# GpSimd's part in a fused cross-attention and coupling-network kernel: low halves in other slots, and five of eight token couplings made on GpSimd

## What is computed

```python
gf = _global_net(x.mean(axis=1, keepdims=True), ...)          # one number for each batch
out = x
for _ in range(3):
    tf = _coupling_net(out, ...)                              # one number for each token
    combined = 0.7 * gf + 0.3 * tf
    coupling = 0.1 + adaptive_range * (combined - 0.5) * 2.0
    out = out + coupling * _twist(out)                        # twist: swap quarters, two of them negated
```

## Time and profile before

| | us |
|---|---|
| median of 3 runs | 1073.47 (1073.15 to 1073.99) |
| the profiled execution | 1072.12 |
| its span, first to last instruction | 1070.2 |
| busy: PE, DVE, ACT, POOL | 977.3, 843.8, 901.5, 573.9 |
| mean granted TensorE clock | 0.983 of full speed |

### The profile page before, as it was taken

One profiled execution on the slowest core, in us unless ns is written; L12 is line 12 of the kernel. 1 busy time (PEld: TensorE's weight loads), 2 busy tenths in 40 slices (PEclk: granted clock), 3 DMA queues, 4 the chain that ended last, 5 costly groups with the idle time before them and its releaser, 6 DMA issues.

```text
span 1070.2 us, 21910 instructions
## 1 busy us (share of the span) xinstructions
PE 977.3 (91%) x7260; PEld 526.2 (49%) x7260; DVE 843.8 (79%) x1770; ACT 901.5 (84%) x1121; POOL 573.9 (54%) x1053
## 2 busy tenths in 40 slices
PE   6899999999899999999999999999989999996993
PEld 4456435554355544555445543555435554454431
DVE  3888796997879886987869879699796988688485
ACT  3999778997799978998789977899779997895575
POOL 3366604876068740887228870487606874087204
PEclk7999999999999999999999999999999999999897
DMA  5433002430033200432005310153002430020002
GB/s 118 88 59 58 6 2 44 103 88 1 1 75 89 71 1 1 98 89 48 1 1 118 88 30 1 36 112 88 0 2 69 92 74 1 2 54 31 11 1 80
DMA packets 191119, 51.71 MB, mean 48 GB/s; under 512 B 165920, under 2 KB 174624, under 8 KB 191008
## 3 DMA queue, kind: packets, MB, share of 16 engines
q1 hardware_dynamic: 191008, 50.31, 22.2%
HBM read 33.37 MB, written 16.78 MB: 47 GB/s over the span
## 4 chain that ended last, share of the span: by engine, by line
PE 43%; DVE 16%; POOL 14%; ACT 13%; issue 10%; SPq 2%; DMA 1%; DVEq 0%; POOLq 0%; ACTq 0%
PE ps L1255 8%; PE ps L1269 7%; PE ps L1239 6%; PE ps L1159 5%; ACT probs L914 5%; PE ps L1190 4%; ACT probs L920 3%; PE ps L1175 3%; POOL f_hat L470 3%; PE ps L1278 2%; POOL twisted L525 2%; DVE move_u L780 2%; DVE move_u L801 2%; DVE move_v L782 2%; POOL q_hat L449 2%
## 5 line engine op out<-in xcount | busy, mean ns | idle before, releaser
L914 ACT ACTIVATE probs<-ps,u_scale 120x2048 f32<-120x2048 f32 x128 | 253.7, 1982 | 23.2 <-PE ps L1159 23.2
L920 ACT ACTIVATE probs<-probs,exp_bias,clip 120x2048 f32<-120x2048 f32 x128 | 270.2, 2111 | 0.1
L1269 PE MATMUL ps<-h,w 128*128 128x512 f32 x384 | 185.5, 605 | 14.5 <-ACT h L948 13.8
L1159 PE MATMUL ps<-q_t,k_t 32*120 32x256 f32 x2048 | 148.9, 405 | 21.5 <-ACT probs L914 20.6
L489 POOL TENSOR_TENSOR c<-tok_c 128x16 f32<-128x16 f32 x8 | 1.8, 223 | 277.8 <-issue 277.8
L1190 PE MATMUL ps<-wo_t,of_t 128*128 128x256 f32 x512 | 143.5, 403 | 1.0 <-DVE xy L717 1.0
L692 DVE STREAM_TRANSPOSE o_t<-ps 128x512 f32<-128x512 f32 x128 | 90.6, 708 | 68.0 <-PE ps L1175 67.7
L1175 PE MATMUL ps<-probs,va 120*32 120x256 f32 x2048 | 138.7, 389 | 1.6 <-ACT probs L920 1.5
L1159 PEld LDWEIGHTS ps<-q_t,k_t 32*120 32x120 f32 x2048 | 93.4, 180 | 58.7 <-issue 51.4
L1269 PEld LDWEIGHTS ps<-h,w 128*128 128x128 f32 x384 | 67.5, 189 | 93.0 <-issue 66.0
L1190 PEld LDWEIGHTS ps<-wo_t,of_t 128*128 128x128 f32 x512 | 86.9, 189 | 49.9 <-issue 41.7
(11 more groups left out here) (132 smaller groups left out, 1791.5 us busy)
## 6 DMA issues: line engine op xcount, KB each, us to landing
xy<-in_x_dram SPq DMA_DIRECT2D x64, 256.0 KB, 3.3
out_dram<-xy SPq DMA_DIRECT2D x64, 256.0 KB, 2.1
cbuf<-in_ctx_dram SPq DMA_DIRECT2D x64, 120.0 KB, 2.8
va<-in_ctx_dram SPq DMA_DIRECT2D x64, 120.0 KB, 3.6
tok_c<-coup SPq DMA_DIRECT2D x256, 0.5 KB, 2.0
move_v<-in_L_xattn_W_out_dram SPq DMA_DIRECT2D x1, 256.0 KB, 5.2
move_u<-in_L_ffn_cn_w_dram SPq DMA_DIRECT2D x1, 256.0 KB, 3.3
w<-in_L_ffn_cn_w_dram SPq DMA_DIRECT2D x1, 128.0 KB, 3.1
```

The source lines that it names most:

```text
L914: eng.activation(probs[:, b % 2, n * HALF:(n + 1) * HALF, :].rearrange("k h q -> k (h q)"), banks(SCORE_BANK, 4)[0:KEYS, :], ACT.Tanh, sca ...
L920: eng.activation(p, p, ACT.Exp, scale=clip[0:KEYS, 0:1], bias=exp_bias[:, b:b + 1]).then_inc(s_exp, 1)
L1159: last = eng.matmul(banks(SCORE_BANK + r)[0:KEYS, odd * S:(odd + 1) * S], k_t[rows, b % 2, odd, n, :], q_t[rows, b % 2, n, :], start=True, ...
L1269: last = eng.matmul(banks(bank), w2[:, k, :], h1[:, p % 2, k, :], start=(k == 0), stop=(k == EK - 1))
```

## The change

GpSimd's low halves of chunks 0 and 1 move from slots 2, 3, 5, 6 to slots 2, 4, 4, 7: of the two in slot 4 one comes right behind the feature norm, the other at the end. And `COUPLE_DVE` = 3: VectorE makes the couplings of updates 0, 1 and 2, GpSimd those of updates 3 to 7, by the same two instructions, between its feature norm of slot 0 and the coefficients. Arithmetic, DMAs and all the other queues are as they were.

```diff
-        LOW_AT = (2, 3, 5, 6)
+        LOW_FIRST = {4: (0, 1)}
+        LOW_LAST = {2: (0, 0), 4: (1, 0), 7: (1, 1)}
+        COUPLE_DVE = CHUNKS - 1
...
+            def couple_beside(g, p):
+
+                turn, chunk = UPDATES * g + p, slot_of(p)[1]
+                eng.wait_ge(s_th, turn + 1)
+                eng.wait_ge(s_gcs, g + 1)
+                eng.wait_ge(s_coup, CB * turn)
+                for b in range(CB):
+                    c = coup[:, turn % 2, b * S:(b + 1) * S]
+                    eng.tensor_scalar(c, c, c_tok[:, 0:1], c_batch[:, chunk * CB + b:chunk * CB + b + 1],
+                                      ALU.mult, ALU.add).then_inc(s_coup, 1)
...
                     norm_2(i - LAG)
+                if place(i) in LOW_FIRST:
+                    low_half((i - LAG) // GROUP, *LOW_FIRST[place(i)])
                 if after_ffn(i):
+                    for p in range(COUPLE_DVE, UPDATES):
+                        couple_beside(groups_before(i) - 1, p)
                     coefficients(groups_before(i) - 1)
...
-                if place(i) in LOW_AT:
-                    part = LOW_AT.index(place(i))
-                    low_half((i - LAG) // GROUP, part // EK, part % EK)
+                if place(i) in LOW_LAST:
+                    low_half((i - LAG) // GROUP, *LOW_LAST[place(i)])
+            for p in range(COUPLE_DVE, UPDATES):
+                couple_beside(NGROUPS - 1, p)
             coefficients(NGROUPS - 1)
...
                     for p in range(CHUNKS):
-                        couple(i, p)
+                        if p < COUPLE_DVE:
+                            couple(i, p)
                         update_both(i, p)
                     for p in range(CHUNKS, UPDATES):
-                        couple(i, p)
                         update_u(i, p)
```

## The result

The changed kernel is slower: 1076.13 us (median of 9 executions, 1075.8 to 1078.9) against 1073.15 for the kernel before in the same measurement. The ratio is 1.0034, with a 95% interval of 1.0023 to 1.0044; on 1073.15 that is 3.6 us (2.5 to 4.7). The predicted time was 1073.9 in a range of 1068.5 to 1078.3. So the time lies in the range, but past the 0.2% that I had called "same", and past the forecast's own range by 0.5 us.

A forecast was written before the change was run, and what follows sets the result against it. In feed-forward, VectorE's updates were taken to hold pass 10's second layer, which sets each group's end. Couplings +1.1 us and low halves -0.7 summed to +0.4, so 1073.47 became 1073.9 us, range 1068.5 to 1078.3.

The forecast's parts named there:

- The bound: Feed-forward stage: the start of pass 10's second layer on TensorE, 543.12, sets the group's end.
- Update 3: Its coupling pair on GpSimd, hidden by nothing, runs 527.2 to 528.3; the moves start 0.5 us later.
- Update 4 and the Gelu of pass 8: VectorE reaches update 4 at 533.95 against 533.90; pass 8's Gelu comes 0.15 us later.
- The size of a half: A GpSimd coupling half takes 1.5 us beside back-to-back VectorE work, 0.55 when VectorE idles; a pair 2.8 us.
- the first rival: GpSimd gets in only when VectorE stops: +4.8 us, with the low halves' move 1077.6; chance 0.22.
- Updates 5 and 6: Update 5's moves 0.1 us earlier; update 6's tanh 0.4 earlier, its moves at 540.35 against 540.26.
- Update 7: Comes 0.4 us later, but its Gelu still precedes TensorE's turn: hidden, except in the last group.
- Part two: Moving the low halves to slots 2, 4, 4, 7 in attention: -0.1 us a group, taken as -0.7 us.
- part one: Five couplings, updates 3 to 7, move from VectorE to GpSimd: +0.1 x 8 + 0.3 = +1.1 us.
- The starved case: Couplings wait for a whole VectorE update, first halves over 2 us; update 6 is 0.55 us later; chance 0.22.
- The whole-instruction lock: VectorE loses the whole 0.55 us per coupling half; update 6 +1.4 us a group, about 1084; chance 0.05.
- The queue really shortens: Coupling pairs near 1.1 to 2 us: -0.3 to -0.7 us a group, 1068 to 1071; chance 0.21.

The follow-up runs named there:

- couple_imm: `couple_only` with GpSimd's coupling instruction taking two constants, 0.05 and 0.1, and no columns; sixth stage 58.19 us against 58.59 before, one execution.
- couple_onecol: `couple_only` with the coupling's scale read from its column and the offset the immediate 0.1; sixth stage 58.42 us against 58.59 before, one execution.
- low_only: The kernel before with only the low halves moved, to slots 2, 4, 4, 7; VectorE makes all couplings; ratio to before 1.0008.
- couple_only: The kernel before with only the couplings of updates 3 to 7 moved to GpSimd, low halves in their old slots; ratio to before 1.0031.
- shadow: The kernel before plus two coupling-form GpSimd instructions on a scratch tile behind each tanh of updates 4 to 7, nobody waiting for them; ratio 1.0068.
- before_rows4: The kernel before with coupling rows in four buffers and four semaphores instead of two, all couplings on VectorE; ratio to before 0.9983.

## Why the prediction was right or wrong

*The bound.* Right: TensorE's second layer of pass 10, held by VectorE's updates through the Gelu, sets the stage's end. It came 0.34 later, and the stage 0.45.

*Update 3.* Right: alone 1.10 us, the moves 0.42 later than before (predicted +0.5). It is one of the two dear steps, +0.34 of the stage.

*Update 4 and the Gelu of pass 8.* Right in number by luck (+0.12 against +0.15). I had VectorE come last, at 533.95, held up by 0.34, and the coupling done by 533.5. VectorE was held up by 0.1 only and free at 533.72, and the pair, 3.35 us and not 2.8, ended at 533.99: two errors met in the same place, and update 4 waited for GpSimd, not for VectorE's own queue.

*The size of a half.* **The step that failed: the length of a coupling half on GpSimd under VectorE's updates.** I took "1.5 us for an instruction while VectorE runs back to back", and four boundaries for a pair, from two normalizations of the same form at 257.30 and 513.92. The halves took 1.34 and 2.02 in update 4, and 2.00 and 0.98 in update 5, the same to 0.02 us in all eight groups. A pair is 3.35 us, not 2.8. `couple_imm` and `couple_onecol` show what it hangs on: the two column operands, without which a half takes 0.97 at most. That each is one more wait for a boundary is inferred. The two rows were of the right form, and no instruction of it in that trace lasted over 1.575 us; why they got through sooner than the 2.0 us of updates 4 and 5 is not shown. The forecast took the longest rows there for the rule and left all that lies above them to the first rival.

*Updates 5 and 6.* Wrong for that reason, twice over. With coupling 4 ending at 533.99 instead of 533.5, GpSimd starts coupling 5 only behind it (the 0.20 in its row), so update 5 is 0.1 late and not 0.1 early. And the rows of coupling 4 land later, so the tanh of update 6 is 0.12 late and not 0.4 early. By the prediction's own steps this 0.5 us passes on to coupling 6 (whose pair was shorter than I had it, 1.79 us for 2.05) and to update 6: +0.34 instead of +0.1. In size this is the whole miss at pass 10: (0.34 - 0.1) x 8 = 1.9 us.

*Update 7.* Wrong: "hidden" it was not. I compared its Gelu with TensorE's turn for pass 11 (546.6 against 547.1), and that part held, as the second layer of pass 11 has no wait. But on ScalarE the second Gelu of pass 10 and the next slot's logits stand behind this Gelu in the queue, so all of its 0.58 us is passed on to them (552.00 - 3.82 = 548.18, was 547.60), and some of it to the last cycle's tanh: the stage ends 0.45 late, not 0.34. This is 0.1 x 8 = 0.9 us. The step asked only who reads the late result, not who is queued behind it.

*Part two.* I had given it 0.1 us a group. `low_only` shows that much for an attention stretch, the changed kernel does not (68.45 us against 68.40 in `couple_only`); ScalarE's idle time is unchanged, as I said. The net was wrong. My row at 507.81 showed that a low half, with its two inputs, can double a VectorE instruction, and I used it only against part one. In slot 7 the moved half did this to `o_n`, and a stage in each of the two kernels was 1.3 to 1.8 us longer behind it.

*The sum.* Part one was to cost 0.1 x 8 + 0.3 = 1.1 us and costs 0.45 x 8 = 3.6 (0.42 x 8 = 3.4 in `couple_only`), part two was to give 0.7 back and gives nothing that can be measured (1.0008, 0.9998 to 1.0017): +0.4 has become +3.6.

*The rivals.* The starved case named +0.55 a group for update 6, and asked for first halves over 2 us. Measured were 1.34, 2.00, 1.25, 1.52 and +0.34: the outcome lies between it and the forecast. The rule of the Trainium skill ("SBUF — State Buffer", "Who interferes with whom") is that the engine which issues first holds the port for its whole length. GpSimd's two-input low half comes near it: `o_n`, begun 0.1 us behind a low half of 1.16, took 1.60 us where it takes 0.70 in the same place of `couple_only`. The couplings do not bear it out: `shadow` shows 0.14 to 0.2 us lost for an instruction that takes 0.55 alone. The whole-instruction lock would have made `shadow` 1.015 or more; it was 1.0068. "The queue really shortens" was true of updates 4 and 5 alone (-0.26 us).

What stays open: how often part two's collision comes, and part of the spread of the last attention stretch, 59.4 to 62.1 us from kernel to kernel. The other part is the clock. In that stretch the granted clock is at its lower level (1.2 GHz) for 6.8 us in eleven traces and for 10.2 us in the three with the longest stretches, 61.7 to 62.1; the 1.9 us between 59.4 (the changed kernel) and 61.2 (before), both with 6.8, are not explained.

## What to carry to other kernels

Before an instruction is handed to a second engine, write down three times for it: when its input is ready, when its reader is free, and how long it lasts *under the stream beside which it will run*; it pays where the lead between the first two covers the third, and here it did for one half (1.8 us) and not for two (3.35). Fewer column operands shorten the last of the three: two less took a half from 2.02 to 0.97 us at most. Splitting a pair so that GpSimd's half was done before VectorE's own took the gain that moving it whole gave away (0.9976 against 1.0011 for updates 4 to 7). And a late result can cost twice: its reader, and everything queued behind the instruction that waits for it.

## What the hardware showed

- On GpSimd a 128x256 `tensor_scalar` beside back-to-back VectorE work takes up to 0.97, 1.47 and 2.02 us with no, one and two column operands, and 0.40, 0.47 and 0.55 alone. Before the result I had given the columns no part in it.
- Each such instruction costs VectorE 0.14 to 0.2 us in `shadow`, where it lasts 0.58 to 2.02 us itself. In the changed kernel ten of them cost VectorE 0.3 us in a whole stage.
- A two-input GpSimd instruction of 1.16 us that started 0.1 us ahead of a VectorE one made that one last 1.60 and 1.65 us instead of 0.97 or less (two cases).
- The profile puts 2.7 us of the tanh's waits in the trace of the kernel before down to row DMAs, in the fifth and seventh stage; some of the 7.0 us that it puts down to `move_u` must be theirs too: the products of update 4 were done at 535.19 (533.90 + 1.29), and the tanh of update 6 began at 537.87. With four buffers (`before_rows4`) none of these waits is left, and the ratio is 0.9983 (0.9974 to 0.9991).
- The granted clock's time at its lower level differs from trace to trace, by 3.4 us and once by 6.8, at the start and in front of the last stage, without regard to where the couplings are made.
